# Edge sums of 128-node tiles with float32r one-hots as weights, and attention's output weights multiplied into the key-value sums once

## What is computed

```python
xn = layernorm(x)
# relational mean: per (relation, destination) the mean of weighted source rows, then that relation's weight
seg  = edge_type * N + dst
sums = segment_sum(xn[src] * edge_weight[:, None], seg, 8 * N)
h    = sums / maximum(segment_sum(1, seg), 1)[:, None]
gnn  = einsum('rnc,rco->no', h.reshape(8, N, 256), weight) + xn @ root + bias
# linear attention over all nodes, 8 heads of 32, f = elu + 1
q, k, v = f(xn @ wq + bq), f(xn @ wk + bk), xn @ wv + bv
kv, ks  = einsum('lhd,lhe->hde', k, v), k.sum(nodes)
att  = einsum('lhd,hde->lhe', q, kv) / (einsum('lhd,hd->lh', q, ks) + 1e-6)[..., None]
x1   = x + gnn + att @ wo + bo
# 6 experts of 3 layers (256 wide), the best 2 of each node weighted by a softmax
f1   = layernorm(x1)
out  = x1 + sum over the node's best two of gate * (relu(relu(f1 @ w1 + b1) @ w2 + b2) @ w3 + b3)
```

## Time and profile before

| | us |
|---|---|
| median of 3 runs | 3860.25 (3853.76 to 3879.67) |
| profiled execution | 3874.72 |
| its span | 3872.9 |

### The profile page before, as it was taken

One profiled execution on the slowest core, in us unless ns is written; L12 is line 12 of the kernel. 1 busy time (PEld: TensorE's weight loads), 2 busy tenths in 40 slices (PEclk: granted clock), 3 DMA queues, 4 the chain that ended last, 5 costly groups with the idle time before them and its releaser, 6 DMA issues.

```text
span 3872.9 us, 58786 instructions
## 1 busy us (share of the span) xinstructions
PE 3508.8 (91%) x19967; PEld 3008.3 (78%) x19968; DVE 1898.3 (49%) x3974; ACT 1437.7 (37%) x2422; POOL 1786.0 (46%) x1841
## 2 busy tenths in 40 slices
PE   5999999966999999988999998998899989899998
PEld 4888888855877778877888777887778877788777
DVE  3477553231554444554455544455455554455544
ACT  4555555520333333333333332333233333333333
POOL 0000000036655655556566555555566656655551
PEclk9999999975998989999899888999899999999989
DMA  5445455453333333333333333333333333333342
GB/s 188 179 189 192 188 195 207 172 181 96 98 100 103 107 97 93 95 102 106 94 96 95 101 101 90 93 94 103 95 105 96 95 103 107 100 89 100 100 86 34
DMA packets 158318, 451.87 MB, mean 117 GB/s; under 512 B 33108, under 2 KB 79098, under 8 KB 138883
## 3 DMA queue, kind: packets, MB, share of 16 engines
q0 software_dynamic: 86400, 236.04, 22.2%
q1 hardware_dynamic: 67836, 205.82, 14.4%
q10 hardware_dynamic: 3546, 3.17, 0.3%
HBM read 301.89 MB, written 143.01 MB: 115 GB/s over the span
## 4 chain that ended last, share of the span: by engine, by line
PE 64%; issue 8%; another core or an unknown queue 2%; DVE 2%; POOL 1%; DVEq 1%; ACT 1%; DMA 0%; ACTq 0%; POOLq 0%
PE bank L1480 37%; PE acc L1488 19%; PE bank L1617 1%; POOL ring L1032 1%; PE acc L1480 1%; PE bank L1463 1%; PE bank L1465 1%; PE acc L1538 1%; PE bank L1570 1%; PE bank L1473 1%; PE bank L1585 0%; DVE res_t L1321 0%; DVE ft_lo L1351 0%; ACT ft_hi L1115 0%
## 5 line engine op out<-in xcount | busy, mean ns | idle before, releaser
L1032 POOL DMA_INDIRECT ring<-y_tab,ring_i x1800 | 1771.4, 984 | 1211.7 <-PE acc L1488 588.9
L1488 PEld LDWEIGHTS acc<-sc,ring 128*128 128x128 f32 x7200 | 899.9, 204 | 176.3 <-issue 168.0
L1488 PE MATMUL acc<-sc,ring 128*128 128x64 f32 x7200 | 906.9, 287 | 126.9 <-issue 65.2
L1102 ACT ACTIVATE h_hi<-bank,bias_t 128x512 fp32r<-128x512 f32 (+1 forms) x600 | 408.4, 681 | 992.5 <-PE bank L1480 494.3
L1316 DVE TENSOR_TENSOR h_lo<-res_t,h_hi 128x512 fp32r<-128x512 f32 (+1 forms) x600 | 406.0, 682 | 668.2 <-ACT res_t L1104 422.2
L711 PE MATMUL yb<-wr_hi,xhl 128*128 128x512 f32 x1568 | 508.5, 395 | 0.0
L1104 ACT ACTIVATE res_t<-bank,bias_t 128x512 f32<-128x512 f32 (+1 forms) x600 | 404.4, 674 | 3.3 <-DVE h_lo L1316 2.8
L1049 POOL COPY ring_i<-idx_t 128x72 int32 x25 | 11.6, 463 | 804.9 <-POOLq L96 804.9
L1480 PE MATMUL bank<-ew_hi,h_hi 128*128 128x256 f32 x1176 | 350.6, 298 | 13.7 <-issue 11.1
L711 PEld LDWEIGHTS yb<-wr_hi,xhl 128*128 128x128 f32 x1568 | 294.3, 188 | 72.1
L1480 PE MATMUL bank<-ew_lo,h_hi 128*128 128x256 f32 x1176 | 337.8, 287 | 12.7 <-issue 12.5
(11 more groups left out here) (246 smaller groups left out, 4804.3 us busy)
## 6 DMA issues: line engine op xcount, KB each, us to landing
y_tab<-yst SPq DMA_DIRECT2D x97, 1024.0 KB, 3.8
ring<-y_tab,ring_i POOLq DMA_INDIRECT x1800
xt_tab<-xhl SPq DMA_DIRECT2D x25, 1024.0 KB, 3.9
xc<-xt_tab SPq DMA_DIRECT2D x25, 1024.0 KB
xs<-in_x SPq DMA_DIRECT2D x24, 512.0 KB, 6.0
x<-in_x SPq DMA_DIRECT2D x24, 512.0 KB
out<-y SPq DMA_DIRECT2D x24, 512.0 KB
stage<-in_L_ffn_expert_w SPq DMA_DIRECT2D x6, 768.0 KB
```

The costliest lines, as they stand in the source:

```text
L1032: pool.indirect_dma_start(out=out_ap, out_offset=None, in_=y_tab[:, :], in_offset=bass.IndirectOffsetOnAxis(ap=idx_ap, axis=0)).then_inc(s ...
L1102: act.activation(dest[:, m, 0:W], b[:, 0:W], ACT.Relu, bias=bias)
L1488: last = pe.matmul(acc[k][:, bass.ds(col, WIN)], rows[:, q, k * P:(k + 1) * P], coefs[:, q, :], start=False, stop=False, skip_group_check= ...
```

## The change

Edge sums become node-major. `acc[h]` now holds two tiles of 128 nodes x 256 features (`sums(t)`). For an edge tile the weights are a float32r one-hot `sel` of 128 edges x 128 nodes; what moves are its gathered rows times the coefficient, as `row_hi` (ACT, `high`) and the rest `row_lo` (DVE, `low_rows`, written over the gathered rows), 256 wide each. Every tile of 128 nodes has 18 edge tiles of its own in the plan, so again 72 a supertile, in 12 portions of 6 with a ring of 3 x 6 tiles in the place of 3 x 8. Portions 0 and 1 come behind `turn`, 2 behind h1 of expert 0, one ahead of each expert's w3, and one more behind the w3 of experts 2, 3 and 4. `row_hi` and `sel` have two buffers each. DVE makes the next supertile's tables, and portion 0 of it, at the end of a pass, before its last adds to `y` (`next_group`), where it made them at the start.

Attention: once, at the start-up, the key-value sums are multiplied by `wo` (`kw_sb`). In a pass the denominators become 8 small products, their reciprocals are spread over each head's 32 features by a copy and eight transposes, the query features are multiplied by them, and `close_sum` is 8 products of 256 columns from query features and `kw_sb`.

Since `acc` is now node-major, the transposes of `res_t`, that tile and its additions go: DVE adds `acc` to x1, to which bias was added in the pass before (`with_bias`). Root products are node-major and wait for that addition. x1 is loaded in two halves. The router's choice on DVE is cut in three (`logits`, `best_two`, `gates`), and gates and the bias of the third layers move from expert 0 to expert 1. In the first stage the tables of the lowest destinations are made by tile, not by block of four tiles, with eight steps of four products in the place of two of four. In the start-up all 12 portions are made ready after the experts' weights are split.

The core of the diff, by engine: constants and tiles, POOL, ACT, DVE (its `iteration` begins with the additions to x1), PE:

```diff
+RANGE = 18
+PT = 6
+PARTS = SUB * RANGE // PT
+SLOTS = 3
+
+AHEAD_W3 = {0: 3, 1: 4, 2: 5, 3: 7, 4: 9, 5: 11}
+BESIDE_W3 = {2: 6, 3: 8, 4: 10}
...
+            with ExitStack() as px:
+                ring = sbuf(px, "ring", [P, SLOTS, PT, C])
+                xring = sbuf(px, "xring", [P, C])
+            row_lo = sbuf(pc, "row_lo", [P, SLOTS, PT, C], F32R)
+            xlo = sbuf(pc, "xlo", [P, C], F32R)
+            row_hi = sbuf(pc, "row_hi", [P, 2, PT, C], F32R)
+            sel = sbuf(pc, "sel", [P, 2, PT, NT], F32R)
...
+            def sums(t):
+                return acc[t // 2][:, (t % 2) * C:(t % 2 + 1) * C]
...
+                def portion(n, p):
+                    pool.wait_ge(portion_used, portions_before(n, p) - SLOTS + 1)
+                    for q in range(PT):
+                        c = p * PT + q
+                        rows(ring[:, p % SLOTS, q, :], ring_i[:, n % 2, c:c + 1], rows_in[p % SLOTS])
...
+                def high(n, p, first=0, end=PT):
+
+                    if first == 0:
+                        act.wait_ge(tab_ready, n + 1)
+                        act.wait_ge(rows_in[p % SLOTS], 16 * PT * ((PARTS // SLOTS) * n + p // SLOTS + 1))
+                        act.wait_ge(portion_used, portions_before(n, p) - 1)
+                    for q in range(first, end):
+                        c = p * PT + q
+                        last = act.activation(row_hi[:, p % 2, q, :], ring[:, p % SLOTS, q, :],
+                                              ACT.Copy, scale=coef_w[:, c:c + 1])
+                    if end == PT:
+                        last.then_inc(hi_ready, 1)
...
                 def iteration(i, plan):
...
                     for e in range(EXPERTS):
-                        hidden("h2", e)
-                        hidden("h1", e + 1)
+                        for m in range(KC):
+                            hidden("h2", e, m)
+                            if more and e in BESIDE_W3:
+                                high(i + 1, BESIDE_W3[e], 3 * m, 3 * m + 3)
+                        if e + 1 < EXPERTS:
+                            for m in range(KC):
+                                hidden("h1", e + 1, m)
...
+                        if more and e + 1 < EXPERTS:
+                            high(i + 1, AHEAD_W3[e + 1])
+                    if more:
+                        for p in range(2):
+                            high(i + 2, p)
 
...
+                def denominators(i, plan):
+                    b = take(i, plan, "den", 0)
+                    gone(dve.tensor_scalar(rden[:, :, :].rearrange("p t h -> p (t h)"), b[:, 0:SUB * HEADS], DEN_EPS, None,
+                                           ALU.add))
+                    dve.drain()
+                    dve.reciprocal(rden[:, :, :], rden[:, :, :])
+                    dve.drain()
+                    dve.tensor_copy(rden_c[:, :, :].rearrange("p t (h d) -> p (t h) d", h=HEADS),
+                                    rden[:, :, :].rearrange("p t h -> p (t h)").unsqueeze(2)
+                                    .to_broadcast([P, SUB * HEADS, C // HEADS])).then_inc(rden_ready, 1)
+
+                def attention(i, plan):
+                    for k in range(KC):
+                        b = take(i, plan, "rd", k)
+                        gone(dve.tensor_tensor(qf[:, k, :], qf[:, k, :], b[:, 0:NS], ALU.mult))
...
                 def tables(n):
...
+                    for t in range(SUB):
+                        lo = dve.value_load(lo_row[0:1, bass.ds(SUB * n + t, 1)], min_val=0, max_val=TILES - RANGE)
+                        cols = slice(t * RANGE, (t + 1) * RANGE)
+                        dve.tensor_scalar(rel_w[:, cols], dst_t[:, bass.ds(lo, RANGE)], base_t[:, t:t + 1], None, ALU.subtract)
+                        last = dve.tensor_copy(coef_w[:, cols], coef_t[:, bass.ds(lo, RANGE)])
...
+                def one_hot(n, p):
+                    dve.wait_ge(portion_used, portions_before(n, p) - 1)
+                    dve.tensor_tensor(sel[:, p % 2, :, :], iota_w[:, :].unsqueeze(1).to_broadcast([P, PT, NT]),
+                                      rel_w[:, p * PT:(p + 1) * PT].unsqueeze(2).to_broadcast([P, PT, NT]), ALU.is_equal)
+
+                def low_rows(n, p):
+                    dve.wait_ge(hi_ready, PARTS * n + p + 1)
+                    for q in range(PT):
+                        c = p * PT + q
+                        last = dve.scalar_tensor_tensor(out=row_lo[:, p % SLOTS, q, :], in0=ring[:, p % SLOTS, q, :],
+                                                        scalar=coef_w[:, c:c + 1],
+                                                        in1=row_hi[:, p % 2, q, :].bitcast(F32),
+                                                        op0=ALU.mult, op1=ALU.subtract)
+                    last.then_inc(lo_ready, 1)
...
+                def next_group(n):
+
+                    leftovers(dve, n - 1, surplus(dve, n - 1), leftover)
+                    next_nodes()
+                    tables(n)
+                    prepare(n, 0)
+
+                def with_bias(i):
+
+                    dve.wait_ge(x1_in, 32 * (i + 1))
+                    dve.tensor_tensor(x1[:, :, :], x1[:, :, :], out_bias[:, :].unsqueeze(1).to_broadcast([P, SUB, C]), ALU.add)
+                    dve.drain()
...
                     for h in range(T // 2):
-                        b = take(i, plan, "x1", h)
-                        gone(dve.tensor_tensor(x1[:, 2 * h:2 * h + 2, :], b[:, :].rearrange("p (t c) -> p t c", t=2),
-                                               x1[:, 2 * h:2 * h + 2, :], ALU.add))
...
+                        dve.wait_ge(acc_full, 2 * i + h + 1)
+                        dve.tensor_tensor(x1[:, 2 * h:2 * h + 2, :], acc[h][:, :].rearrange("p (t c) -> p t c", t=2),
+                                          x1[:, 2 * h:2 * h + 2, :], ALU.add).then_inc(x1_done, 1)
+                        dve.drain()
+                        for t in (2 * h, 2 * h + 1):
+                            dve.bn_stats(stats[:, t, :], x1[:, t, :])
                     dve.drain()
                     for t in range(T):
...
-                        build(i + 1, 0)
+                        one_hot(i + 1, 1)
...
-                    route(i, plan)
+                    logits(i, plan)
                     if more:
-                        further(1, lo, far)
+                        prepare(i + 1, 3)
...
+                        if e == 0:
+                            gates(i, plan)
+                        if more and e == 1:
+                            denominators(i, plan)
+                        if more and e in BESIDE_W3:
+                            prepare(i + 1, BESIDE_W3[e])
+                        if more and e == 2:
+                            attention(i, plan)
                         if more and e == EXPERTS - 1:
-                            further(EXPERTS + 1, lo, far)
+                            next_group(i + 2)
                         if e == 0:
                             dve.wait_ge(y_stored, 16 * (i + 1))
...
+                        if more and e + 1 < EXPERTS:
+                            prepare(i + 1, AHEAD_W3[e + 1])
+                        if more and e == EXPERTS - 2:
+                            with_bias(i + 1)
...
+                def root(i, plan):
+                    for t in range(SUB):
+                        if plan is LOOP and t % 2 == 0:
+                            pe.wait_ge(x1_done, 2 * i + t // 2 + 1)
+                        nodes = slice(t * NT, (t + 1) * NT)
+                        last = in_parts(sums(t), lambda k: xc[:, 0, k, nodes], lambda k: xc[:, 1, k, nodes],
+                                        lambda k: wqr_hi[:, 1, k, :], lambda k: wqr_lo[:, 1, k, :], more=True, begin=t % 2 == 0)
                     return last
...
+                def denominators(i, plan):
+                    b = give(i, plan, "den", 0)
+                    pe.wait_ge(qf_ready, KC * (i + 1) + KC)
+                    half = HEADS // KC
+                    for t in range(SUB):
+                        for k in range(KC):
+                            last = pe.matmul(b[:, t * HEADS + k * half:t * HEADS + (k + 1) * half],
+                                             qf[:, k, t * NT:(t + 1) * NT], ksum_h[:, k, :], start=True, stop=True)
+                    filled(last)
+
+                def spread(i, plan):
+                    for k in range(KC):
+                        b = give(i, plan, "rd", k)
+                        pe.wait_ge(rden_ready, i + 2)
+                        for t in range(SUB):
+                            last = pe.transpose(b[:, t * NT:(t + 1) * NT],
+                                                rden_c[:, t, k * P:(k + 1) * P], ident[:, :])
...
+                def aggregate(n, p):
+
+                    pe.wait_ge(lo_ready, PARTS * n + p + 1)
+                    into = sums(p * PT // RANGE)
+                    for q in range(PT):
```

(53 more changed lines are left out.)

691 lines of the change are left out of this document (266 added, 425 removed).

## The result

| us | kernel before | changed kernel |
|---|---|---|
| median | 3869.96 (3853.76 to 3887.29, 4 runs) | 4200.88 (4174.84 to 4202.76, 4 runs) |
| span of the profiled execution | 3872.9 | 4201.0 |

The account below looks back on a forecast made before the run. TensorE in the loop bounded the old kernel; the new pass's chain of waits, 108.0 us plus 4.5 for clock, made 113. 972 + 24 x 113 + 46 = 3730, less 12.6 of profiled span over median: 3717 us, range 3570 to 3880.

Parts of the forecast that it names:

- expert 1: End of expert 1 in the new pass's chain, after a wait, denominators, gates and b3: 42 us.
- portions 6, 8, 10: Second portions of experts 2, 3 and 4, 15.2 us each from h2's start, bringing the chain to 87.6.
- last split of expert 5: Chain of the pass: expert 5's h2 (2.8) and split of its second half (2.3), ending at 92.7 us.
- next pass, with the clock's 4.5: Chain end at 108.0 us, plus a tenth extra on 45 us of matmul for a granted clock of 0.90: 113.
- a doubling of the 38 ns: Gathers' mean excess of 38 ns beside DVE operations, if doubled: POOL needs 100.5 us a pass, the ring 106.
- the rival with a third of the gathers waiting 1.3 us each: Gathers blocked through six low-rows operations: 31 us on POOL's 97.7, a pass of 129, 4101 us; chance 8%.
- The ring of 18: Gather ring cut from 24 tiles to 18, portion 3's gathers waiting for portion 0's use: 103 us, second to 113.
- The rival of "no gain": Ring and seam between passes add up instead of lying beside each other: 113 + 6 = 119, 3861 us; chance 14%.
- these delays are in the 119.9 too: Argument against the late-signals rival: the old kernel's measured pass of 119.9 us already contains such delays.
- The rival "PE's signals come late": Late TensorE signals at seven hand-overs, decisive from 1 us each; at 2 a pass is 127, 4053 us; chance 10%.
- the two rows that showed it: ACT's h_hi released 78 times by no engine's work, 170 us; DVE starting 4.3 us after the close's modelled end.
- The seam from DVE's last split to the next pass: End of a pass: DVE's next tables, one-hot, low rows, adding y and the branch back, 15.3 us.

Follow-up runs that it names:

- after_again_2: Changed kernel run again unaltered, on a chip where the kernel before took about 3700 and no signals came late: 3789.58 us, ratio 1.030.
- before_kw: Kernel before with only attention changed: wo multiplied into key-value sums at start-up, no numerator products; 3659.17 us against 3696.50, ratio 0.989.
- no_gather: Changed kernel without its gathers, POOL only signals and scaled rows come from a constant tile: 3587.95 us where the kernel before took 3932.
- gather_unread: Changed kernel with all gathers landing in a tile nobody reads, row_lo double-buffered: 3590.75 us where signals are on time, 4129.47 where late.

## Why the prediction was wrong

**Right, by its own steps.** The chain of one pass holds where signals are on time. Forecast and measured ends (changed kernel, 116.0 us a pass; but for the last row the forecast is at full clock, the measured ends are at the clock granted):

| step | forecast | measured |
|---|---|---|
| transposes of the normalised tile | 7.5 | 7.1 |
| h2 of expert 0 begins | 17.7 | 17.2 |
| portion 3 | 24.6 | 27.7 |
| expert 1 | 42 | 45.2 |
| portions 6, 8, 10 | 57.2, 72.4, 87.6 | 60.3, 75.8, 92.6 |
| last split of expert 5 | 92.7 | 98.6 |
| next pass, with the clock's 4.5 | 113 | 116.0 |

Edge sums run at 0.12 us a product without gaps, the waits ahead of portions 6, 8 and 10 are low rows, and TensorE is busy for 81% of the loop. Copies on ACT start each 0.41 us, not 0.49.

**The gathers beside DVE.** They take 1.06 us in the mean (1.09 where signals are on time), where a doubling of the 38 ns would have been 1.02. POOL's own work came out as forecast all the same: 100.4 us a pass where signals are on time (116.0 less the 15.6 in which it waits for a portion to be used), against 100.5. So the rival with a third of the gathers waiting 1.3 us each (8%, 31 us a pass) is out: they grew by 8 to 10 (72 times 0.115 and 0.142). But its mechanism is in the trace. A gather can be held by several operations in a row, here low rows and then the bias:

```profile
3074.14 1.67 DVE L1227 SCALAR_TENSOR_TENSOR row_lo<-ring,coef_w,row_hi 128x256 fp32r<-128x256 f32 x4
...
3074.95 2.81 POOL L1020 DMA_INDIRECT ring<-y_tab,ring_i  x1 [0.30 <-issue]
...
3075.72 1.22 DVE L1261 TENSOR_TENSOR x<-x,out_bias 128x1024 f32<-128x1024 f32 x1
```

It ends 0.82 us after the bias. In after_again_2, 456 of the 458 gathers longer than 1.15 us end 0.82 us after such an operation. So did the 3.46 us gather of the earlier trace rows, at 871.24 against 870.42 for L1409; the prediction read it as ending with that operation, and took one operation as the most that can hold a gather. The Trainium skill, "SBUF — State Buffer", section "Who interferes with whom", says that a VectorE instruction with two SBUF inputs contends with a GpSimd one that reads SBUF. The trace agrees.

**The term that was mis-sized: the ring.** The ring of 18 was called second to the chain, at 103 us beside 113. (Its own terms add up to 105.4, which changes nothing.) But it isn't a bound beside the chain. It adds at one place: portion 3's gathers begin when portion 0 is used (8.8), and end at 18.4. Their copies are ready at 22.8 and the low rows at 25.3, and behind those in DVE's queue stands h2's split of expert 0. That is the 3.1 us at portion 3, and smaller waits follow; together 116.0 - 109.5 = 6.5 us a pass. The rival of "no gain" had this mechanism at 6 us, and its place was the seam, not portion 3.

**The step that failed: the 119.9 us and what hides in them.** The prediction took TensorE's late signals as part of the pass before and priced the new chain at modelled ends: "these delays are in the 119.9 too". That is the argument that failed. On other chips the kernel before takes 3697 to 3706. No profile of it was taken there; its span of 3704.2 less the 972.8 us that before_kw spends outside its loop gives an estimate of 113.8 us a pass. With no gathers it is 113.0. So some 6 of the 119.9 were late signals, and against 113.8 the forecast of 113 was hardly a gain. The new kernel pays more for them: 132.66 - 116.05 = 16.6 us a pass, 400 us in all. The rival "PE's signals come late" had the mechanism, at 10% (18% for all that is slower), but not the shape: it priced 2 us at each of seven hand-overs (127 us, 4053). Measured, 11.7 of the 16.6 us are lost by the end of portion 4 (51.8 against 40.1), and some 5 in all the rest of the pass. It should have been the first of the cases: the two rows that showed it were in the text.

**Why the new kernel pays more.** That the short portions left the hand-overs uncovered is an argument, not shown: no run lengthened a portion again, and the one slow place speaks for more than that. Shown is that the loss needs gathers in flight (109.5 without, 131.7 with, unread), more than 36 a pass, and a chip on which signals come late.

**The rest.** The loop begins 22 us later than before, 23 forecast. Where signals are on time it is about 34 (960.0 against 925.7 in before_kw). The seam from DVE's last split to the next pass takes 17.4 us, 15.3 forecast, and is on the chain, but no more than the rest of DVE's list. The one part of attention that was run alone gains 37 us. All the rest of the change (node-major edge sums, the small denominators, the longer start-up) loses some 130 us where signals are on time: 3789.58 against 3659.17, from two chips on which the kernel before agrees to about 1 us. Which of them loses it was not separated.

## What to carry to other kernels

- When an engine's signals are late in the trace (idle time that ends with no engine's work, a consumer that starts microseconds after the modelled end), price the new chain with that delay, and don't take it for a constant part of the old time. Here it grew from some 6 to 16.6 us a pass while TensorE's work shrank. And most of it lay in one place, not at every hand-over.
- A ring isn't only a rate. Follow the first transfer that its size delays to what stands behind it in the consumer's queue.
- Run the kernel before beside every experiment. Here two chips disagree on one program by 15%, and only the neighbour tells which of them it was.

## What the runs showed of the hardware

- Late signals and slow issue belong to a chip. On one chip (and wherever the first runs were made) the kernel before took 3870 to 3930 us, on four others 3697 to 3706; the traces with 72 gathers a pass have them on the former. With 36 gathers, with none, or with copies on POOL in their place, TensorE has no `issue` row and no engine a `remote` one there (1100 to 3500 us). Of the ten traces taken on the latter none has a `remote` row in that stretch, and only the one of 7567 us has an `issue` row of TensorE, once, 1.0 us. The granted clock doesn't set the two apart: no_gather was granted 0.935 on the former, gather_unread 0.940 on the latter, in nearly the same time. All gathers unread: 4129 and 3591 us for the same program.
- They aren't a queue of transfers: with late signals as without, a gather's last packet ends 1.5 us after its instruction (median of 1812, both chips). What it is that backs up these traces don't show.
- With a small copy and a drain on POOL behind each gather, POOL stands idle for 2.3 us ahead of the next one, 0.30 without.
- A gather beside VectorE operations with two SBUF inputs is held until 0.82 us after one of them ends, and several in a row can hold it: 2.81 us, where one alone takes 0.95.
